# Edges that start and end at the same node leave a graph kernel's edge machinery

## The reference, cut to what matters

```python
def _spmm_plus_eye(rows, cols, vals, X):
    msgs = vals[:, None] * X[cols]
    agg = jax.ops.segment_sum(msgs, rows, num_segments=N)
    return agg + X
...
support = feature @ W1
out = _spmm_plus_eye(rows, cols, vals, support)
out = _batchnorm_relu(out, gamma, beta)
out = _spmm_plus_eye(rows, cols, vals, out @ W2)
...
x = x + gnn(layernorm(x), src, dst, edge_weight, W1, W2, gamma, beta)
x = x + moe(layernorm(x))     # 8 experts of 256 x 256 twice, the best 2 of 8 weighted
```

## Time and profile before

| | |
|---|---|
| median of 3 runs | 4853.54 us (4851.01 to 4862.56) |
| span of the profiled execution, first to last instruction | 4441.9 us |
| median less span | 411.6 us |
| busy, share of the span | PE 86%, PEld 76%, DVE 82%, ACT 72%, POOL 66% |
| moved by DMA | 912 MB |

### The profile page before, as it was taken

One profiled execution on the slowest core, in us unless ns is written; L12 is line 12 of the kernel. 1 busy time (PEld: TensorE's weight loads), 2 busy tenths in 40 slices (PEclk: granted clock), 3 DMA queues, 4 the chain that ended last, 5 costly groups with the idle time before them and its releaser, 6 DMA issues.

```text
span 4441.9 us, 89077 instructions
## 1 busy us (share of the span) xinstructions
PE 3835.3 (86%) x28089; PEld 3367.7 (76%) x28089; DVE 3642.4 (82%) x10236; ACT 3212.7 (72%) x6844; POOL 2932.2 (66%) x3137
## 2 busy tenths in 40 slices
PE   1688888888879898898689999999999998999998
PEld 1688888888867777776368888878778887888888
DVE  8789888889968888788568888888888888888886
ACT  3699988889977777777357666766676666666665
POOL 0466766767756666564777777777777777777761
PEclk6799999999989999999579999999999999999999
DMA  9788888888788989896534444444444444444331
GB/s 259 280 322 317 328 317 316 327 312 299 294 306 309 313 307 306 306 320 219 175 108 122 117 127 116 122 117 126 117 122 117 127 118 121 117 126 118 111 102 31
DMA packets 325097, 912.01 MB, mean 205 GB/s; under 512 B 49990, under 2 KB 136095, under 8 KB 322127
## 3 DMA queue, kind: packets, MB, share of 16 engines
q0 software_dynamic: 150336, 475.32, 32.5%
q1 hardware_dynamic: 172119, 417.55, 28.6%
q10 hardware_dynamic: 2172, 13.35, 0.8%
HBM read 575.92 MB, written 330.10 MB: 204 GB/s over the span
## 4 chain that ended last, share of the span: by engine, by line
PE 41%; DVE 21%; DMA 12%; ACT 11%; issue 8%; POOL 6%; SPq 0%; ACTq 0%; DVEq 0%; POOLq 0%
PE ps L1651 8%; PE ps L1672 7%; DMA msgd<-A,tabT 5%; POOL G L1470 4%; DMA G<-h,tabT 4%; PE ps L1394 4%; ACT A L922 3%; PE ps L1542 3%; DVE S L1340 3%; DVE low L1344 3%; PE ps L1125 2%; PE ps L826 2%; PE ps L857 2%; PE ps L1546 2%; PE ps L1544 2%
## 5 line engine op out<-in xcount | busy, mean ns | idle before, releaser
L1470 POOL DMA_INDIRECT G<-h,tabT x1530 | 1505.3, 984 | 523.9 <-issue 362.3
L922 ACT ACTIVATE A<-ps,A 128x256 f32<-128x256 f32 x1856 | 745.8, 520 | 78.2 <-PE ps L858 75.9
L973 POOL DMA_INDIRECT msgd<-A,tabT x464 | 570.4, 1229 | 333.9 <-ACT A L922 230.1
L1523 ACT ACTIVATE gH<-G,tabT 128x256 fp32r<-128x256 f32 x1020 | 496.1, 504 | 352.6 <-DMA G<-h,tabT 335.8
L1502 DVE SCALAR_TENSOR_TENSOR gL<-G,tabT,gH 128x256 fp32r<-128x256 f32 x1020 | 485.9, 476 | 150.1 <-ACT gH L1523 148.6
L857 PE MATMUL ps<-winH,DT 128*128 128x256 f32 x1856 | 511.9, 307 | 51.1 <-issue 35.1
L1490 DVE TENSOR_SCALAR s<-iota,tabT 128x125 fp32r<-128x125 f32 x1700 | 546.8, 335 | 0.8
L858 PE MATMUL ps<-winL,DT 128*128 128x256 f32 x1856 | 471.8, 286 | 0.0
L1544 PE MATMUL ps<-gH,s 128*125 128x256 f32 x1134 | 366.7, 325 | 82.0 <-ACT gH L1523 57.7
L857 PEld LDWEIGHTS ps<-winH,DT 128*128 128x128 f32 x1856 | 361.4, 195 | 68.3 <-issue 48.7
L1751 ACT ACTIVATE ps<-ps,b1T 128x500 f32<-128x500 f32 (+1 forms) x432 | 264.3, 612 | 167.3 <-PE ps L1651 165.8
(11 more groups left out here) (317 smaller groups left out, 11198.3 us busy)
## 6 DMA issues: line engine op xcount, KB each, us to landing
L<-msgd SPq DMA_DIRECT2D x300, 520.0 KB, 5.9
L<-msgd SPq DMA_DIRECT2D x100, 650.0 KB, 5.9
A<-sbd SPq DMA_DIRECT2D x58, 805.0 KB, 6.6
msgd<-A SPq DMA_DIRECT2D x100, 390.0 KB
G<-h,tabT POOLq DMA_INDIRECT x1530
winR<-h SPq DMA_DIRECT2D x116, 128.0 KB
A<-in_x SPq DMA_DIRECT2D x10, 1120.0 KB
h<-A ACTq DMA_DIRECT2D x10, 1120.0 KB
```

The source lines that it names most:

```text
L922: e.activation(M[:, n, 0:F], psum[4 + v % 4][:, (n % 2) * F:(n % 2 + 1) * F], ACT.Identity, scale=M[:, n, F + 2:F + 3]).then_inc(evc, 1)
L973: e.indirect_dma_start(msgd, bass.IndirectOffsetOnAxis(ap=idxI[g % 4][:, t:t + 1], axis=0), msg[g % 3][:, t * 4 * RW:(t + 1) * 4 * RW], No ...
L1470: e.indirect_dma_start(B.G[c % GRL], None, of, bass.IndirectOffsetOnAxis(ap=tab3[:, m, 0:1].bitcast(I32), axis=0)).then_inc(gatl[c % GRL], 16)
L1523: e.activation(B.gH[c % HR2][:, :], B.G[c % GRL], ACT.Identity, scale=w_).then_inc(g_hi, 1)
```

## The change

An edge with equal ends does not need a message: its term is weight x the node's own row. The change adds up these weights d per node and multiplies: `acc * (1 + d) + psum` in both sums. In the begin stage DVE compares `rS` with `rD`, and gives such edges a block number of 100 or more, which no block matches, so that they are not ranked. Their weight reaches its node in the product of `pe_place`, which has four columns more: `dve_place` writes them with one more operation, `dve_record` reduces five columns for four. SP stores 128 sums per group to a DRAM array (`loops`); two arrays are used in turn, since windows of neighbouring groups overlap. At the end they are loaded, added and transposed by PE into `own1`.

With 12,514 edges fewer, a group holds GE2 = 1968 edges for 1840, so there are G2 = 108 groups for 116; each block has 16 main chunks for 17 (pieces of 4, 4, 4, 4), and ten blocks share a tail for five. Worked out from the drawn input, all conditions of the flag hold: at most 2036 of 2048 slots in a group, at most 69 of 128 in a tail, and windows two groups apart start at least 214 nodes apart.

```diff
-KC = 18
+KC = 17
...
-TB = 5
+TB = 10
...
-GE2, JC, JP = 1840, 16, 115
-G2 = 116
+GE2, JC, JP = 1968, 16, 123
+G2 = 108
...
-PIECES = [(b, k, n) for b in range(NB) for k, n in ((0, 5), (5, 4), (9, 4), (13, 4))]
+PIECES = [(b, k, PC) for b in range(NB) for k in range(0, KM, PC)]
...
-FIRST = [0, 10, 18, 26]
+FIRST = [2 * PC * p for p in range(4)]
...
+            for k in range(2):
+                e.dma_start(loopd[k].rearrange("(p n) o -> p (n o)", p=R), zrow[0:R, 0:NB]).then_inc(fillm, 16)
...
-            ready()
-            e.tensor_copy(sbb, rB).then_inc(sbr, 1)
-            e.scalar_tensor_tensor(rS, rB, -float(R), rS, ALU.mult, ALU.add).then_inc(edg, 1)
             e.wait_ge(ld_dst, 48)
             own.done(e.tensor_copy(rD, rDI))
             ready()
+            own.done(e.tensor_tensor(sbb, rS, rD, ALU.is_equal))
+            ready()
+            e.scalar_tensor_tensor(rS, rB, -float(R), rS, ALU.mult, ALU.add).then_inc(edg, 1)
+            e.wait_ge(edg, 1)
+            for p in range(8):
+                c_ = slice(p * EIGHTH, (p + 1) * EIGHTH)
+                own.done(e.scalar_tensor_tensor(rB[:, c_], sbb[:, c_], float(NB + p), rB[:, c_], ALU.mult, ALU.max))
+            ready()
+            e.tensor_copy(sbb, rB).then_inc(sbr, 1)
...
+            own.done(e.tensor_scalar(loop, bS, NB - 0.5, None, ALU.is_gt))
+            own.done(e.tensor_scalar(q4, V4[:, :, :, 0, :], -4.0, 256.0, ALU.mult, ALU.add))
+            ready()
+            own.done(e.tensor_tensor(eqS, eqS, loop, ALU.mult))
+            ready()
+            own.done(e.tensor_tensor(corr, corr, eqS, ALU.add))
...
+            e.tensor_tensor(V[:, :, 112:VC, :].rearrange("p h (v t) l -> p h v t l", t=5)[:, :, 0:3, 4, :],
+                            vals[:, g * 7 * JC:(g + 1) * 7 * JC].rearrange("p (h v l) -> p h v l", h=8, v=7)[:, :, 4:7, :],
+                            loop[:, g * JC:(g + 1) * JC].rearrange("p (h o l) -> p h o l", h=8, o=1).broadcast_to([JP, 8, 3, 2]),
+                            ALU.mult).then_inc(spr, 1)
...
-                m = e.matmul(psum[1][:, 0:P], O[:, j // 2, :, j % 2], V[:, j // 2, :, j % 2], start=j == 0, stop=j == JC - 1)
+                m = e.matmul(psum[1][:, 0:VC], O[:, j // 2, :, j % 2], V[:, j // 2, :, j % 2], start=j == 0, stop=j == JC - 1)
...
-                r0 = PADN + b * STRIDE + KLO * P
-                e.dma_start(msgd[r0:r0 + 3 * P, :].rearrange("(p k) r -> p (k r)", k=3), zrow).then_inc(fillm, 16)
+                r0 = PADN + b * STRIDE + FROW
+                e.dma_start(msgd[r0:r0 + STRIDE - FROW, :].rearrange("(p k) r -> p (k r)", k=4), zrow[0:(STRIDE - FROW) // 4]).then_inc(fillm, 16)
+
+            def loops(g):
+                e.wait_ge(recd, 3 * (g + 1))
+                _, v = nc.values_load_multi_w_load_instructions(
+                    r0I[0:1, g:g + 1], engines=[e.engine], min_val=0, max_val=N - P,
+                    skip_runtime_bounds_check_because="a node's number, at most N - P by a minimum")
+                e.dma_start(loopd[g % 2][bass.ds(v[0], P), :], idf[g][:, 4:5]).then_inc(st_sb, 16)
...
+            e.wait_ge(ld_pre, 64 + 32)
+            e.tensor_tensor(loopT[0], loopT[0], loopT[1], ALU.add).then_inc(vio, 1)
+            e.wait_ge(vsum, 3)
+            own.done(e.tensor_scalar(own1, psum[0][0:R, 128:128 + NB], 1.0, None, ALU.add))
...
-                    e.tensor_tensor(acc_b(b), acc_b(b), psum[b % 2][0:R, 0:F], ALU.add).then_inc(r_add, 1)
+                    e.scalar_tensor_tensor(acc_b(b), acc_b(b), own1[:, b:b + 1], psum[b % 2][0:R, 0:F], ALU.mult, ALU.add).then_inc(r_add, 1)
...
-                        e.tensor_tensor(a, a, psum[b % 2][0:R, 0:F], ALU.add).then_inc(g_add, 1)
+                        e.scalar_tensor_tensor(a, a, own1[:, b:b + 1], psum[b % 2][0:R, 0:F], ALU.mult, ALU.add).then_inc(g_add, 1)
```

More of the change, by code:

```diff
@@ L55 @@
 ZROW = RMAX + PADN + 8
-NDUMP = 3
-GFILL = 92
+NDUMP = 5
+GFILL = 90
 FILL0 = 10
 MW = 16 * RW
+VC = P + 4
 WC = 96
@@ L195, in build @@
     sbd = nc.dram_tensor("sbd", (1, G2 * GE2), BF16, kind="Internal").ap()
+    loopd = [nc.dram_tensor(f"loopd{k}", (N, 1), F32, kind="Internal").ap() for k in range(2)]
     def msg_piece(b, k, n):
@@ L218, in build @@
         pre = sb("pre", [36, P])
-        small = sb("small", [P, 968])
-        tabT = sb("tabT", [P, 3 * NCF])
+        small = sb("small", [P, 1068])
+        tabT = sb("tabT", [P, max(3 * NCF, 5160)])
         psum = [ctx.enter_context(nc.psum_tensor(f"ps{i}", [P, 512], F32)) for i in range(8)]
@@ L235, in build @@
         phase = ExitStack()
-        A = Cut(phase.enter_context(nc.sbuf_tensor("A", [P, 34300], F32)))
+        A = Cut(phase.enter_context(nc.sbuf_tensor("A", [P, 34620], F32)))
         def half(n, p=P):
             return A((n + 1) // 2, p).bitcast(BF16)
-        SBRF = [half(2 * G2 * JC) for i in range(3)]
+        SBRF = [half(max(2 * G2 * JC, BE)) for i in range(3)]
         SBR = [t[:, 0:BE] for t in SBRF]
@@ L246, in build @@
         corr = half(G2 * JC, JP)
-        VV = [half(P * JC, JP) for i in range(2)]
+        VV = [half(VC * JC, JP) for i in range(2)]
         T1 = half(JC * JC, JP)
@@ L304, in build @@
         diag = cut(G2, G2)
-        idf = [cut(4) for i in range(2)]
+        idf = [cut(5) for i in range(G2)]
+        loop = cut(G2 * JC // 2, JP).bitcast(BF16)
+        loopT = [cut(R, NB) for i in range(2)]
         idxI = [cut(4).bitcast(I32) for i in range(4)]
@@ L339, in build @@
         tail125 = small[:, 46:46 + TB]
-        tailN = small[0:NB, 52:53]
+        tailN = small[0:NB, 60:61]
+        own1 = small[0:R, 968:968 + NB]
         tailW = small[0:1, 76:77]
@@ L547, in dve_constants @@
                 own.done(e.memset(t, 0.0))
+            for t in VV:
+                own.done(e.memset(t.rearrange("p (h c l) -> p h c l", h=8, l=2)[:, :, VC - 1:VC, :], 0.0))
             own.done(e.tensor_copy(onesb, ones))
@@ L1006, in sp_messages @@
                     fill(FILL0 + g)
+                if g >= 2:
+                    loops(g - 2)
+            for g in range(G2 - 2, G2):
+                loops(g)
+            e.wait_ge(st_sb, 16 * (G2 + 1))
+            for k in range(2):
+                e.dma_start(loopT[k], loopd[k].rearrange("(b p) o -> b (p o)", p=R)).then_inc(ld_pre, 16)
         def scattered(e):
@@ L1075, in dve_verdict @@
             worst(5, base[:, G2:G2 + 1], KC * P - 3)
-            worst(6, base[:, G2:G2 + 1], KLO * P, ALU.min, ALU.is_lt)
+            worst(6, base[:, G2:G2 + 1], FROW, ALU.min, ALU.is_lt)
+            starts = r0z[0:1, :].rearrange("p (g k) -> p g k", k=2)[:, :, 0]
+            own.done(e.tensor_tensor(tmpv[0:1, 0:G2 - 2], starts[:, 2:G2], starts[:, 0:G2 - 2], ALU.subtract))
+            ready()
+            own.done(e.tensor_reduce(vtmp[0:1, :], tmpv[0:1, 0:G2 - 2], AX.X, ALU.min))
+            ready()
+            own.done(e.tensor_scalar(viol[0:1, 11:12], vtmp[0:1, :], float(P), None, ALU.is_lt))
+            ready()
             for i, (g, n) in enumerate(EARLY):
@@ L1104, in pe_verdict @@
             e.matmul(psum[0][:, 16:16 + NB + 1], ones[0:NB, :], tailL, start=True, stop=True).then_inc(vsum, 1)
+            e.wait_ge(vio, 3)
+            e.transpose(psum[0][0:R, 128:128 + NB], loopT[0], ident[0:NB, 0:NB]).then_inc(vsum, 1)
         def pe_dense1_y(e, i, aT):
@@ L1258, in sp_read @@
             for u, (b, k, n) in enumerate(PIECES):
-                if k == PC + PC - 1 and b == 0:
+                if k == 2 * PC and b == 0:
                     acc_load(e, 0)
```

44 lines of the change are left out of this document (22 added, 22 removed).

## The result

The changed kernel takes 5178.25 us (median of 4 runs, 5175.34 to 5203.2), the kernel before 4852.27 in the same session: ratio 1.0671, interval 1.0648 to 1.0694. The prediction was 4631 us, faster. The sign is wrong.

A forecast was written before the change was run, and what follows sets the result against it. Messages and read had no single leader (PE, DVE, DMA engines all busy); the last stage ran at POOL's gather pace. Terms 5 - 60 - 38 - 130 = -223 gave span 4219, time 4631 us; 8-in-10 range 4590 to 4700.

The forecast's parts named there:

- The small stores: Messages: 128 writes of 4 bytes per group were put at no cost, since DMA engines have 15% left.
- Rival 3: Messages: small writes load the DMA engines, 1.06 us a group, +114, 4746 us; chance 0.05, beyond that price 0.02.
- the point of 2.06 us a group: Messages: store price per group above which the changed kernel gets slower than before, 0.26 us for each 4-byte write.
- an upper end: Messages: 132 ns per small write, from SP's queue's mean packet, taken as highest price: 1.06 us of all engines per group.
- The time around the span: Whole kernel: 411.6 us around the profiled span of 4441.9 us, taken as unchanged; result put against the median 4853.5 us.
- Begin, +5: Begin stage: DVE's added work before the layernorm +2.8 us, the weights' tables +2; sum +5, bounds 0 and +8.
- the +2.8 worked out: Begin: later layernorm start from DVE's added comparison, small operations and 7% wider work, less what the narrower padding gives back.
- The narrower padding: Begin: padding 44 wide, not 940, lets the three waiting loads start some 2.6 us earlier.
- Messages, -60: Messages: eight groups fewer -76.5 us, DVE's extra work +16, small stores nothing; bounds -77 and -29.
- Read, -38: Read stage: one of 17 main chunks goes, -40; multiply-add and tails +2; bounds -28 and -45.
- Last, -130: Last stage: 16.1 gathers a block for 17.2 at POOL's pace, -130 us on 92 blocks, -5 on others, 5 given back.
- Rival 1: Last stage: PE becomes the bound, staying at 92.6% busy; 92 blocks save 60 us, plus 5; time 4696; chance 0.12.

The follow-up runs named there:

- the kernel with 64-byte stores: Kernel before plus 128 stores of 64 bytes side by side per group, which nobody reads; stand-in for before in 4855 sessions; ratio 1.0007 to before.

## Why the prediction was wrong, point by point

**The small stores: the step that failed.** "In the sum they cost nothing, since the engines have 15% left" is the step that failed: the term was put at nothing, and it is 4.4 to 4.6 us per group in the kernel before, and 4.1 in the changed one (the flag at 1677.5 us for 1232.0 with the sums stored once, over 108 groups). Where before takes 4855 us, the changed kernel stands at 1.067 with them and at 0.973 with its sums stored once; where it takes 4440, at 0.951 without them and at 0.952 with its sums stored once. Before with the stores alone stands at 1.104 and 1.118. Rival 3 had the right place and the right sign: "longer waits for scatters mean rival 3", and the point of 2.06 us a group from which it decides. Its price was more than four times too low, and its chance, 0.02 beyond that price, was worked out from "the mean packet of SP's queue", 132 ns, called "an upper end". It was not one: it bounded what the stores' own packets take, and these do take little (11 ns). What it left out is what they do to the packets of the scatters' queue, of which there are 573 per group. A row on a queue's packets in a stretch without such writes says nothing on that.

The rule of the Trainium skill ("DMA: Bandwidth & Descriptors", Specifications), by which transfers below 512 B are read-modify-writes and miss line rate, pointed at the right line of the diff. These runs agree that such a write can be dear, but the size alone doesn't tell: 4 and 8 bytes well apart, and 64 side by side, are all below 512 B and cost nothing (ratios 1.0003, 1.0006, 1.0007). Why the writes to the same 64 bytes hold up the scatters' queue, no record shows; that the DMA engines each write a part of it and must take turns is my reading, not shown.

**The time around the span.** "The 411.6 us around it are taken as unchanged": they don't exist (4438.97 us against a span of 4437.2). It didn't change the sign, but the base of every steady window was a session that the times weren't from. This fault matters too: with the stores out of the way, the time in a 4855 session is 4730.66 us, which is still above the range's upper end of 4700.

**Begin, +5.** The first statistics of the layernorm now start at 29.83 us, not 23.87:

```profile
9.77 1.19 DVE L526 CAST raw<-raw 108x1968 f32<-108x1968 int32 x1 [8.16 <-DMA raw<-in_src]
...
29.83 0.42 DVE L649 BATCH_NORM_STATS2 small<-A 125x6 f32<-125x256 f32 x1
```

That is +6.0 for the +2.8 worked out. The narrower padding was to give 2.6 us back; but the edges land at 9.77 us where they landed at 9.93, although SP now issues their load at 1.12 us in place of 3.95. So the padding wasn't what they were late by; what was, is open. The wait before L526 is 8.16 us now, 5.67 before.

**Messages, -60, without the stores.** The pace of 9.7 us came as 9.63. Begin and messages together were to give -55; without the stores or with one store at the end the flag comes 45 us earlier (1212.0 and 1212.3 for 1257.0), inside the bounds, and 49 us in the 4855 sessions (1232.0 for 1280.6).

**Read, -38.** 81 multiply-adds of the sum in 600 us are 7.4 us a block (7.55 expected):

```profile
L1423 DVE SCALAR_TENSOR_TENSOR acc<-acc,small,ps 125x256 f32<-125x256 f32 x81 | 38.1, 470 | 0.3 <-PE ps L1453 0.3
```

It takes 0.47 us, as estimated from the last stage's. From the flag to the first set, which holds the read and four blocks of the last stage, both sessions give -45 to -51 without the stores.

**Last, -130.** Near it where its rows came from, and inside its bounds: -108 and -118 us from the first to the last set, POOL at its own pace (waits of 0.3 us). In the session of the times it is -26, because POOL waits for PE there. Rival 1 named that wait, but its saving of 65 us for this stage was still too much: PE doesn't stay at 92.6% but at 85%. What makes PE slower in those sessions is open. Rows of the kernel with 64-byte stores show PE's longest waits; the pauses "issue" are those for which the profile has no releaser. The clock in the same window is 0.91:

```profile
PE ps L1685 <- DVE X L1931: 53.3, 21, 5.0
PE ps L1685 <- issue: 38.1, 61, 5.6
```

In the 4440 session PE's longest waits in this stage are all for ACT or DVE, of 40 us and less in 1768. Whether the pauses bring the lower clock or the clock the pauses, these rows don't tell.

## What to carry to other kernels

A store from 128 partitions of one value each is 128 writes into 512 bytes, and in these runs the scatters that the DMA engines carried at that time paid its price: 4.1 us each, 445 us in all, for 54 KB of sums. Keep such columns in SBUF, transpose them on PE and write rows, or at least put the values 64 bytes apart. Look at the median and the longest packets too: here a mean that nearly doubled came from one packet in sixteen. When a diff adds a kind of transfer that no row of the trace shows, its bound from above isn't the mean packet; what it may do to the other queues is unbounded by any row, and one experiment with the stores alone settles it. And compare the span with the times before anything else: here they were 411.6 us apart because they were of different sessions, and the engine that bounds a stage in one did not bound it in the other.

## What was unexpected of the hardware

- 128 writes of 4 bytes side by side, in 9.6 us of steady traffic, raise the mean packet of another queue from 151 to 287 ns, while the DMA engines' busy share goes up from 0.85 to 0.96 and the rate down from 315 to 218 GB/s. Their own packets show 11 ns. The other queue's median stays at 161 ns for 4160 bytes; 6% of its packets last 1 to 7 us.
- The effect is gone at one write per 64 bytes, and 0.24 us per 128 writes at four per 64 bytes, against 4.4 at sixteen.
- PE's granted clock fell from 0.97 to 0.82 in the messages as it waited more, though no instruction of PE was changed there but for four more columns (with the stores alone and none changed, to 0.79).
- The same kernel takes 4440 or 4855 us from session to session, with most of the difference in the last stage (2390.0 us from the first to the last set in the kernel that stands for it, for 2048.2).
